# Token loop of a transformer block: order of five calls on TensorE and two on VectorE

## The chip, the cores and the metric

The kernel runs on one core of a Trainium2 chip. The metric is the device time of one execution in microseconds (us), lower is better. The engines named here are TensorE (PE in the profile, its weight loads apart as PEld), VectorE (DVE), ScalarE (ACT), GpSimd (POOL) and the DMA queues.

## The reference

The input is 32 sequences of 64 tokens, 256 wide, so 2048 tokens in 16 tiles of 128. The reference computes, in this order:

- a mixture of experts: top two of eight experts per token, three matrix products each (256 to 512 to 512 to 256);
- layer one, attention with 16 heads of 64: `q, k, v = tanh(m @ W + b)`, causal softmax, `ctx`, and `x1 = x + tanh(ctx @ Wo + bo)`;
- layer two, attention with 16 heads of 16, whose probabilities are scaled by a coherence factor and mixed with a field term (`mod = (1 - fi) * mod + fi * fa`), then `a = out @ Wout.T + bout`;
- a feed-forward step on quantised numbers: `a` is rounded in blocks of 32 to an FP4 grid, giving rows `xq`, and the result is `x1 + xq @ w_q.T + bias`.

## The kernel before

The first part computes the experts over sorted token slots. The second part, the token loop, is the subject. It takes the 16 tiles one after the other as a software pipeline written out by hand: in iteration t, TensorE does the projections, values and scores of layer one for tile t, the context of layer one for tile t-1, most of layer two for tile t-2, and the turn (transpose) of the quantised rows and the feed-forward product for tile t-3. The loop `for t in range(2, TT + 3)` at the end of TensorE's program runs t from 2 to 18; calls whose tile does not exist do nothing, so iterations 16, 17 and 18 run down with fewer and fewer calls. VectorE and ScalarE have their own lists of calls in their own loops. Every engine works its list in order, and waits on semaphores join the lists; there is no scheduler.

The calls and lines that matter:

- `l1_v(t, s)`, L870: values of layer one, tile t, sequence half s. Four matmuls in the code, two of them side by side on the two 64-column halves of the array (`tile_position=(0, r * SEQ)`), 512 columns of data each. Half 0 writes bank 3, half 1 bank 0. Half 0 waits for ScalarE's tanh of the first group of `k` projections, half 1 for that of the second.
- `l2_turn_p(t - 2, n)`, helper line L895: four turns of 128x128 of layer two's shares `p2`; n = 0 waits for the shares, n = 1 for VectorE's result of the tile before (L1889). The same helper line serves `l1_turn_p`. What is turned is copied with the field term added by VectorE's `l2_field` (L1862), for which `l2_context` (L1017) waits.
- `l2_v(t - 2)`, L980: values of layer two, on 64-column halves too; waits for VectorE's `l2_shift` (L1831). VectorE's `l2_v` (L1815) adds the bias.
- `l2_turn_q(t - 3)`, L1035: two bf16 turns of 128x128 of the quantised rows `xq`; waits for the last operation of VectorE's `l2_round` (L1416). ScalarE copies the result (`l2_xqt`, L1335), for which the product `l2_ffn` (L1044) waits.
- `l1_context` (L920) on 64x64 tiles, `l1_out` (L929), `l1_scores` (L888), the projections `l1_q` and `l1_k` (L844), the scores of layer two (L995).
- `tail_busy(t, last, n)`, L1051: n matmuls of no use, issued in iteration `last` alone: in iteration 17 the counts are 44, 12 and 26, in iteration 18 it is 84.

A 32-bit matmul of the code is two MATMUL instructions in the profile, so that `l1_v` shows x8 there and x4 in the program's order below; `l2_turn_p` is x4 in both.

Of the kernel before, what the change touches and what calls it, by code (L numbers as in the profile page):

```python
# [95 lines left out]
def exists(t, n):  # L96

    return not isinstance(t, int) or 0 <= t < n
# [12 lines left out]
def value_bank(t, s):  # L111

    return (1, 2)[s] if t == 0 else (3, 0)[s]
# [46 lines left out]
def build(nc, t_in, out):  # L160
    ctx = ExitStack()
    with ctx:
# [456 lines left out]
        def _(pe):  # L619
# [203 lines left out]
            def halves():  # L823

                return [(s, slice(s * SEQ, (s + 1) * SEQ)) for s in range(2)]

            def l1_turn_m(t):
                if not exists(t, TT):
                    return
                pe.wait_ge(m_set, t + 1)  # L830
                if t > 1:
                    pe.wait_ge(exp1_set, 2 * t)
                elif t == 0:
                    pe.wait_ge(h1t_set, SLOT_TILES)
                for k in range(KH):
                    last = pe.transpose(ps[:, turn_bank(t), k * P:(k + 1) * P], m_rows[:, k * P:(k + 1) * P], ident[:, :])
                last.then_inc(mt_ps, 1)

            def l1_project(t, wt, n):
                b = project_bank(t, n)  # L840
                for c in range(4):
                    f = (n * 4 + c) * P
                    for k in range(KH):
                        last = mm(ps[:, b, c * P:(c + 1) * P], wt[:, k, f:f + P], m_t[:, k, :],  # L844
                                  start=k == 0, stop=k == KH - 1)
                last.then_inc(qk_ps, 1)

            def l1_q(t, n):
                if not exists(t, TT):
                    return  # L850
                if n == 0:
                    pe.wait_ge(mt_set, t + 1)
                l1_project(t, wq, n)

            def l1_k(t, n):
                if not exists(t, TT):
                    return
                pe.wait_ge(qk_set, 4 * t + n + 1)
                l1_project(t, wk, n)

            def l1_v(t, s):
                if not exists(t, TT):
                    return
                if t:
                    pe.wait_ge(qk_set, 4 * t + 3 + s)
                if t == 1:
                    pe.wait_ge(exp1_set, 1 + s)
                for k in range(KH):
                    for r in range(2):
                        last = mm(ps[r * SEQ:(r + 1) * SEQ, value_bank(t, s), :], m_t[:, k, s * SEQ:(s + 1) * SEQ],  # L870
                                  wv[:, k, r * 512:(r + 1) * 512], start=k == 0, stop=k == KH - 1,
                                  tile_position=(0, r * SEQ))
                last.then_inc(v_ps, 1)
# [18 lines left out]
            def turn_p(p, bank_, n, done):  # L892
                for m in range(4):
                    h = 8 * n + 2 * m
                    last = pe.transpose(bank_[:, m * P:(m + 1) * P], p[:, h:h + 2, :], ident[:, :])  # L895
                last.then_inc(done, 1)
# [76 lines left out]
            def l2_v(t):  # L973
                if not exists(t, TT):
                    return
                pe.wait_ge(u2_set, 2 * t + 2)
                for s, q in halves():
                    for k in range(KH):
                        for r in range(2):
                            last = mm(ps[r * SEQ:(r + 1) * SEQ, 6, s * P:(s + 1) * P], x1_t[:, k, q],  # L980
                                      wv2[:, k, r * P:(r + 1) * P], start=k == 0, stop=k == KH - 1,
                                      tile_position=(0, r * SEQ))
                last.then_inc(v2_ps, 1)
# [15 lines left out]
            def l2_turn_p(t, n):  # L999
                if not exists(t, TT):  # L1000
                    return
                if n == 0:
                    pe.wait_ge(p2_set, t + 1)
                elif t:
                    pe.wait_ge(fin_set, t)
                turn_p(p2, T2[n], n, pt2_ps)
# [23 lines left out]
            def l2_turn_q(t):  # L1030
                if not exists(t, TT):
                    return
                pe.wait_ge(xq_set, t + 1)
                for k in range(KH):
                    last = pe.transpose(turned_q[:, k, :], xq[:, k * P:(k + 1) * P], ident_h[:, :])  # L1035
                last.then_inc(xqt_ps, 1)
# [11 lines left out]
            def tail_busy(t, last, n):  # L1048
                if t == last:
                    for _ in range(n):  # L1050
                        mm(bank(0, P), ident_h[:, :], ident_h[:, :], start=True, stop=True)  # L1051
# [32 lines left out]
            for t in range(2, TT + 3):  # L1084
                tail_busy(t, TT + 2, 84)
                l1_turn_m(t)
                l2_hidden(t - 2)
                l2_q_or_k(t - 2, 5, wk2)
                l1_q(t, 0)
                l2_coherence(t - 2)  # L1090
                l2_scores(t - 2)
                tail_busy(t, TT + 1, 44)
                l1_q(t, 1)
                l1_turn_p(t - 1, 0)
                l1_k(t, 0)
                l1_turn_p(t - 1, 1)
                l1_k(t, 1)
                l2_v(t - 2)
                tail_busy(t, TT + 1, 12)
                l2_turn_q(t - 3)  # L1100
                l1_context(t - 1)
                l2_ffn(t - 3)
                tail_busy(t, TT + 1, 26)
                l1_v(t, 0)
                l2_turn_p(t - 2, 0)
                l1_v(t, 1)
                l2_turn_p(t - 2, 1)
                l1_out(t - 1)
                l2_context(t - 2)
                l1_scores(t)  # L1110
                l1_turn_x1(t - 1)
                l2_out(t - 2)
                l2_q_or_k(t - 1, 4, wq2)
# [273 lines left out]
        def _(dve):  # L1387
# [242 lines left out]
            def l1_mix(t):  # L1630
                if not exists(t, TT):
                    return
                dve.wait_ge(y_gathered, 16 * TOPK * (t + 1))
                if t:
                    dve.wait_ge(mt_ps, t)
                step(ts(m_rows, yg[:, 0, :], weight_of[:, 0, t:t + 1], None, ALU.mult))
                stt(m_rows, yg[:, 1, :], weight_of[:, 1, t:t + 1], m_rows, ALU.mult, ALU.add).then_inc(m_set, 1)  # L1637
# [109 lines left out]
            def l1_v(t, s):  # L1747
                if not exists(t, TT):
                    return
                dve.wait_ge(v_ps, 2 * t + s + 1)  # L1750
                tt(v[:, s, :], bank(value_bank(t, s)), half_row("bv"), ALU.add).then_inc(vb_set, 1)
# [8 lines left out]
            def l1_sums(t):  # L1760
                if not exists(t, TT):
                    return
                step(red(z1, e1, X, ALU.add))
                step(dve.reciprocal(r1, z1))
# [90 lines left out]
            def l2_field(t, n):  # L1855
                if not exists(t, TT):
                    return
                if t == 0:
                    dve.wait_ge(field_loaded, 16)
                share = field_t[:, t:t + 1, :].to_broadcast([P, 4, P])  # L1860
                dve.wait_ge(pt2_ps, 2 * t + n + 1)
                tt(pt2[:, 4 * n:4 * n + 4, :], T2[n].rearrange("p (m q) -> p m q", m=4), share, ALU.add  # L1862
                   ).then_inc(pt2_set, 1)
# [27 lines left out]
            for t in range(0, TT + 3):  # L1891
                if t:
                    l1_mix(t)
                l2_field(t - 3, 0)
                l1_v(t - 1, 1)
                l2_field(t - 3, 1)
                l2_x1_bias(t - 3)
                l1_bias_o(t - 2)
                l1_residual(t - 2)
                l1_mask(t - 1, 0)  # L1900
                l2_bias_a(t - 3)
                l1_mask(t - 1, 1)
                l1_sums(t - 1)
                l2_scales(t - 3)
                l1_share(t - 1)
                l2_max(t - 2, 0)
                l2_z(t - 2)
                l2_max(t - 2, 1)
                l2_coherence(t - 2)
                l2_shift(t - 2, 0)  # L1910
                l2_shift(t - 2, 1)
                l2_round(t - 3)
                l2_sums(t - 2)
                l2_v(t - 2)
                l2_share(t - 2)
                l1_ctx(t - 1, 0)
                l2_result(t - 3)
                l1_v(t, 0)
                l1_ctx(t - 1, 1)
# [71 lines left out]
```

## Time and profile before

| | us |
|---|---|
| median of 3 runs | 776.12 |
| the three runs | 777.77, 776.09, 776.12 |
| the profiled execution, device time | 777.57 |
| its span, first to last instruction | 775.8 |
| PE busy | 738.0 (95%) |
| DVE busy | 497.4 (64%) |
| ACT busy | 281.0 (36%) |
| mean granted TensorE clock (1 is 2.4 GHz) | 0.98 |

The token loop takes the second half of the span, from about 320 us on. Its full iterations last close to 27 us each. A timeline row gives the start of a group of equal instructions, the time from its start to its end, the engine, the line, the operation and tiles, and in brackets the idle time ahead of it with what ended it. The end of a matmul row overlaps the start of the next, so the time that a group takes is read from start to start.

### The profile page before, as it was taken

The page shows a single profiled execution, that of the slowest core. Times are in us where ns is not written, and L with a number is a line of the kernel's source. Part 1 is how long each engine was busy: PE and PEld are TensorE (multiplying, and loading weights), DVE is VectorE, ACT ScalarE, POOL GpSimd, SP SyncE. Part 2 cuts the span into 40 slices and gives each one's busy share as a digit, 9 for nine tenths or more (in the row PEclk, how much of TensorE's full clock was granted, in tenths as well). Part 3 has the DMA queues.
Part 4 walks back from the last instruction along what each step waited for, and adds up shares of the span by engine and source line. Part 5 has one row for each costly group of instructions (what it writes and reads, how often), then busy time and mean ns, then how long its engine had stood idle before and what let it go on. Part 6 is the DMA issues. An engine that isn't in the chain of part 4 may idle for free.

```text
span 775.8 us, 22474 instructions
## 1 busy us (share of the span) xinstructions
PE 738.0 (95%) x9282; PEld 625.6 (81%) x9282; DVE 497.4 (64%) x1099; ACT 281.0 (36%) x823; POOL 84.8 (11%) x95
## 2 busy tenths in 40 slices
PE   6289999999999999999999999999999999999886
PEld 3189999569999999778977887797788779778775
DVE  3846665745444444247777877877787788678756
ACT  3032212241221221345633643563465346435420
POOL 2121112511111101110000000000000000000000
PEclk9599999999999999999999999999999999999899
DMA  9787311316110103210000000001000000000000
GB/s 317 272 270 265 131 33 44 102 42 245 41 42 29 42 22 114 78 33 5 23 29 22 10 29 29 15 16 30 22 15 23 29 22 10 29 16 9 8 9 15
DMA packets 29586, 49.27 MB, mean 64 GB/s; under 512 B 3307, under 2 KB 19051, under 8 KB 28973
## 3 DMA queue, kind: packets, MB, share of 16 engines
q1 hardware_dynamic: 20432, 32.47, 12.2%
q0 software_dynamic: 3744, 10.49, 4.5%
q10 hardware_dynamic: 5309, 4.87, 1.9%
q8 instruction: 74, 1.21, 0.7%
q14 instruction: 27, 0.22, 0.1%
HBM read 41.00 MB, written 6.82 MB: 62 GB/s over the span
## 4 chain that ended last, share of the span: by engine, by line
PE 87%; DMA 6%; DVE 4%; SPq 1%; issue 1%; ACT 1%; DVEq 0%; POOL 0%; POOLq 0%
PE ps L743 15%; PE ps L844 15%; PE ps L777 7%; PE ps L929 7%; PE ps L713 7%; PE ps L870 7%; DMA arena<-in_w 5%; PE ps L895 4%; PE ps L949 3%; PE ps L920 2%; PE ps L888 2%; PE ps L980 2%; PE ps L961 2%; PE ps L1027 2%; PE ps L995 2%; PE ps L1044 2%
## 5 line engine op out<-in xcount | busy, mean ns | idle before, releaser
L844 PE MATMUL ps<-arena,l_weights 128*128 128x128 f32 x1024 | 125.8, 276 | 0.0
L743 PE MATMUL ps<-h_t,w_now 128*128 128x128 f32 x1056 | 123.5, 275 | 1.0 <-DVE h_t L1611 1.0
L743 PEld LDWEIGHTS ps<-h_t,w_now 128*128 128x128 f32 x1056 | 120.5, 192 | 1.3 <-issue 1.2
L844 PEld LDWEIGHTS ps<-arena,l_weights 128*128 128x128 f32 x1024 | 119.3, 192 | 1.1
L1169 ACT ACTIVATE h_t<-ps,cols 128x128 f32<-128x128 f32 x132 | 37.7, 368 | 167.9 <-issue 149.4
L1586 DVE COPY w_now<-arena 128x2048 f32 x33 | 40.5, 1227 | 81.2 <-PE ps L743 70.8
L1240 ACT ACTIVATE arena<-ps,cols 128x128 f32<-128x128 f32 x256 | 73.1, 371 | 19.4 <-PE ps L844 19.4
L610 POOL DMA_INDIRECT arena<-expert_out,slot_of x32 | 30.6, 956 | 357.6 <-DVE arena L1637 308.9
L713 PEld LDWEIGHTS ps<-xg_t,w_now 128*128 128x128 f32 x528 | 63.4, 192 | 5.2 <-ACT xg_t L1152 2.6
L713 PE MATMUL ps<-xg_t,w_now 128*128 128x128 f32 x528 | 65.1, 276 | 2.0 <-DVE w_now L1572 1.5
L579 POOL DMA_INDIRECT xg<-in_x,slot_tok x36 | 41.3, 1147 | 193.4 <-PE ps L692 161.7
L777 PE MATMUL ps<-arena,h_t 128*128 x264 | 62.4, 379 | 0.0
L870 PE MATMUL ps<-l_weights,arena 128*64 128x512 f32 x256 | 61.8, 604 | 0.0
L1274 ACT ACTIVATE arena<-arena 128x256 f32<-128x256 f32 x16 | 6.7, 416 | 146.7 <-DVE arena L1783 146.7
L929 PE MATMUL ps<-l_weights,arena 128*128 128x256 f32 x256 | 58.1, 380 | 0.1
L929 PEld LDWEIGHTS ps<-l_weights,arena 128*128 128x128 f32 x256 | 47.4, 190 | 7.0 <-DVE arena L1776 1.2
L777 PEld LDWEIGHTS ps<-arena,h_t 128*128 128x128 f32 x264 | 47.6, 190 | 5.1
L895 PEld LDWEIGHTS ps<-ident,arena 128*128 128x128 f32 x256 | 29.3, 145 | 24.4 <-issue 22.7
L1572 DVE COPY w_now<-arena 128x1024 f32 x33 | 23.1, 699 | 34.0 <-PE ps L713 21.0
L895 PE MATMUL ps<-ident,arena 128*128 128x128 f32 x256 | 41.1, 286 | 0.6 <-DVE arena L1853 0.5
L1611 DVE TENSOR_SCALAR h_t<-ps,cols 128x128 f32<-128x128 f32 x132 | 37.0, 342 | 4.1 <-PE ps L743 4.0
L870 PEld LDWEIGHTS ps<-l_weights,arena 128*64 128x64 f32 x256 | 15.6, 136 | 24.4 <-issue 24.1
(301 smaller groups left out, 1110.0 us busy)
## 6 DMA issues: line engine op xcount, KB each, us to landing
arena<-in_w SPq DMA_DIRECT2D x16, 512.0 KB, 7.2
arena<-in_w SPq DMA_DIRECT2D x8, 1024.0 KB, 6.6
expert_out<-y ACTq DMA_DIRECT2D x36, 128.0 KB, 1.7
arena<-in_x_t SPq DMA_DIRECT2D x2, 1024.0 KB, 6.0
arena<-in_x SPq DMA_DIRECT2D x16, 128.0 KB, 2.3
out<-arena SPq DMA_DIRECT2D x16, 128.0 KB, 1.7
b<-in_b SPq DMA_DIRECT2D x1, 1024.0 KB, 13.1
l_weights<-in_wq SPq DMA_DIRECT2D x1, 1024.0 KB, 4.9
```

Of the source, the lines that this page charges most:

```text
L579: pool.indirect_dma_start(out=xg[j % XG][:, :], out_offset=None, in_=t_in["x"], in_offset=bass.IndirectOffsetOnAxis(ap=slot_tok[:, slot_ti ...
L713: last = mm(ps[:, 0, m * P:(m + 1) * P], w1_now[:, k, m * P:(m + 1) * P], xg_t[:, k, :], start=k == 0, stop=k == KH - 1)
L743: last = mm(ps[:, 2, m * P:(m + 1) * P], w2_now[:, k, m * P:(m + 1) * P], h1_t[j % 2][:, k, :], start=k == 0, stop=k == KM - 1)
L777: last = mm(bank(4, HID), h2_t[j % 2][:, k, :], flat[:, bass.ds(at + k * HID, HID)], start=k == 0, stop=k == KM - 1)
L844: last = mm(ps[:, b, c * P:(c + 1) * P], wt[:, k, f:f + P], m_t[:, k, :], start=k == 0, stop=k == KH - 1)
L870: last = mm(ps[r * SEQ:(r + 1) * SEQ, value_bank(t, s), :], m_t[:, k, s * SEQ:(s + 1) * SEQ], wv[:, k, r * 512:(r + 1) * 512], start=k == ...
L895: last = pe.transpose(bank_[:, m * P:(m + 1) * P], p[:, h:h + 2, :], ident[:, :])
L929: last = mm(bank(1, HID), ctx_t[:, c, :], wo[:, c, :], start=c == 0, stop=c == C1 - 1)
L1169: last = f(h1_t[j % 2][:, k, :], ps[:, 0, k * P:(k + 1) * P], ACT.Relu, bias=cols[:, bass.ds(e * KM + at + k, 1)])
L1240: last = f(dst[:, cc, :], ps[:, project_bank(t, n), c * P:(c + 1) * P], ACT.Tanh, bias=col(bias)[:, cc:cc + 1])
L1586: dve.tensor_copy(w2_now[:, :, :].rearrange("p k n -> p (k n)"), arena[:, bass.ds(at, KM * MID)]).then_inc(w2_set, 1)
L1611: last = ts(h2_t[j % 2][:, k, :], ps[:, 2, k * P:(k + 1) * P], cols[:, bass.ds(e * KM + at + k, 1)], 0.0, ALU.add, ALU.max)
```

## The change

Two pairs of calls change places in TensorE's loop, and one in VectorE's to match. Nothing is added or removed, and every call keeps its waits.

```diff
@@ TensorE, for t in range(2, TT + 3)
                 l1_turn_p(t - 1, 1)
                 l1_k(t, 1)
+                l2_turn_q(t - 3)
                 l2_v(t - 2)
                 tail_busy(t, TT + 1, 12)
-                l2_turn_q(t - 3)
                 l1_context(t - 1)
                 l2_ffn(t - 3)
                 tail_busy(t, TT + 1, 26)
                 l1_v(t, 0)
+                l1_v(t, 1)
                 l2_turn_p(t - 2, 0)
-                l1_v(t, 1)
                 l2_turn_p(t - 2, 1)
                 l1_out(t - 1)
@@ VectorE, for t in range(0, TT + 3)
                     l1_mix(t)
+                l1_v(t - 1, 1)
                 l2_field(t - 3, 0)
-                l1_v(t - 1, 1)
                 l2_field(t - 3, 1)
```

TensorE's order in a full iteration, before, from the last projection (L844) to the output of layer one (L929):

```order
L844 MATMUL ps<-arena,l_weights 128x128 x8
L980 MATMUL ps<-arena 64x128 x8
L1035 MATMUL ps<-before,arena 128x128 x2
L920 MATMUL ps<-arena 64x64 x32
L1044 MATMUL ps<-wffn,arena 128x256 x6
L870 MATMUL ps<-l_weights,arena 64x512 x4
L895 MATMUL ps<-ident,arena 128x128 x4
L870 MATMUL ps<-l_weights,arena 64x512 x4
L895 MATMUL ps<-ident,arena 128x128 x4
L929 MATMUL ps<-l_weights,arena 128x256 x8
```

The same place in the changed kernel:

```order
L844 MATMUL ps<-arena,l_weights 128x128 x8
L1035 MATMUL ps<-before,arena 128x128 x2
L980 MATMUL ps<-arena 64x128 x8
L920 MATMUL ps<-arena 64x64 x32
L1044 MATMUL ps<-wffn,arena 128x256 x6
L870 MATMUL ps<-l_weights,arena 64x512 x8
L895 MATMUL ps<-ident,arena 128x128 x8
L929 MATMUL ps<-l_weights,arena 128x256 x8
```

The turn L1035 now follows the projection, which has its shape; the two halves L870 and the two groups of turns L895 have each become one run.

TensorE's order in iteration 17, where tiles run out, before:

```order
L1051 MATMUL ps<-before 128x128 x44
L980 MATMUL ps<-arena 64x128 x8
L1051 MATMUL ps<-before 128x128 x12
L1035 MATMUL ps<-before,arena 128x128 x2
L1044 MATMUL ps<-wffn,arena 128x256 x6
L1051 MATMUL ps<-before 128x128 x26
L895 MATMUL ps<-ident,arena 128x128 x8
```

and in the changed kernel:

```order
L1051 MATMUL ps<-before 128x128 x44
L1035 MATMUL ps<-before,arena 128x128 x2
L980 MATMUL ps<-arena 64x128 x8
L1051 MATMUL ps<-before 128x128 x12
L1044 MATMUL ps<-wffn,arena 128x256 x6
L1051 MATMUL ps<-before 128x128 x26
L895 MATMUL ps<-ident,arena 128x128 x8
```

The values L980 and the twelve fillers behind them now stand behind the turn L1035 and its wait.

On VectorE, at the start of an iteration, the difference between before (-) and the changed kernel (+) is:

```order
 L1637 SCALAR_TENSOR_TENSOR arena<-arena,weight_of 128x256
-L1862 TENSOR_TENSOR arena<-ps,arena 128x512
-L1751 TENSOR_TENSOR arena<-ps,half_rows 128x512
-L1862 TENSOR_TENSOR arena<-ps,arena 128x512
+L1751 TENSOR_TENSOR arena<-ps,half_rows 128x512
+L1862 TENSOR_TENSOR arena<-ps,arena 128x512 x2
 L1798 TENSOR_TENSOR arena<-arena,rows 128x256
```

The bias of the second value half (L1751) goes ahead of the first field sum (L1862). ScalarE's order is the same.

## Rows read from the trace of the kernel before

**Rows 1.** Busy time by engine in stretches: a full iteration; iteration 16's low-clock stretch.

```profile
507.00:534.00 27.00, 27.00 (x438) 22.20 (x440) 20.64 (x44) 13.37 (x41) 1.89 (x2) 1.00 0.08 22
...
729.80:740.00 10.20, 8.05 (x99) 6.24 (x100) 9.72 (x24) 3.65 (x7) 0.00 (x0) 0.50 0.02 4
```

**Rows 2.** Timeline of PE, full iteration: values, turns, output.

```profile
524.70 1.94 PE L870 MATMUL ps<-l_weights,arena 128*64 128x512 f32 x8
526.57 0.66 PE L895 MATMUL ps<-ident,arena 128*128 128x128 f32 x4
527.16 1.94 PE L870 MATMUL ps<-l_weights,arena 128*64 128x512 f32 x8
529.03 0.66 PE L895 MATMUL ps<-ident,arena 128*128 128x128 f32 x4
529.52 3.62 PE L929 MATMUL ps<-l_weights,arena 128*128 128x256 f32 x16
```

**Rows 3.** Timeline of PE ahead of the loop: tile 0's two value halves together.

```profile
322.56 3.65 PE L870 MATMUL ps<-l_weights,arena 128*64 128x512 f32 x16
326.14 1.16 PE L888 MATMUL ps<-arena 64*64 64x64 f32 x64
```

**Rows 4.** Timeline of PE, next full iteration: projections, turns, layer two's values.

```profile
544.40 1.95 PE L844 MATMUL ps<-arena,l_weights 128*128 128x128 f32 x16
546.19 0.60 PE L895 MATMUL ps<-ident,arena 128*128 128x128 f32 x4
546.62 1.95 PE L844 MATMUL ps<-arena,l_weights 128*128 128x128 f32 x16
548.50 1.09 PE L980 MATMUL ps<-arena 128*64 128x128 f32 x16
549.53 0.28 PE L1035 MATMUL ps<-before,arena 128*128 128x128 bf16 x2
549.74 0.46 PE L920 MATMUL ps<-arena 64*64 64x64 f32 x16
```

**Rows 5.** Timeline of DVE, the same iteration: last operation of the rounding.

```profile
547.83 0.42 DVE L1416 TENSOR_TENSOR arena<-arena 128x256 bf16<-128x256 f32 x1
```

**Rows 6.** Timeline of PEld, iteration 16: weight load of the turn.

```profile
735.89 0.13 PEld L1035 LDWEIGHTS ps<-before,arena 128*128 128x128 bf16 x2 [1.18 <-DVE arena L1416]
```

**Rows 7.** Timeline of PE, iteration 16.

```profile
733.14 1.98 PE L980 MATMUL ps<-arena 128*64 128x128 f32 x16 [1.29 <-DVE arena L1831]
735.90 0.40 PE L1035 MATMUL ps<-before,arena 128*128 128x128 bf16 x2 [0.78 <-DVE arena L1416]
736.23 1.99 PE L920 MATMUL ps<-arena 64*64 64x64 f32 x64
738.15 1.46 PE L1044 MATMUL ps<-wffn,arena 128*128 128x256 bf16 x6
739.45 1.65 PE L895 MATMUL ps<-ident,arena 128*128 128x128 f32 x8
741.04 3.72 PE L929 MATMUL ps<-l_weights,arena 128*128 128x256 f32 x16
```

**Rows 8.** Timeline of DVE, iteration 16: last operation of the rounding.

```profile
735.42 0.42 DVE L1416 TENSOR_TENSOR arena<-arena 128x256 bf16<-128x256 f32 x1
```

**Rows 9.** Timeline of PE, iteration 17.

```profile
752.61 2.63 PE L1051 MATMUL ps<-before 128*128 128x128 bf16 x44
756.16 1.09 PE L980 MATMUL ps<-arena 128*64 128x128 f32 x16 [0.92 <-DVE arena L1831]
...
758.92 0.28 PE L1035 MATMUL ps<-before,arena 128*128 128x128 bf16 x2 [0.89 <-DVE arena L1416]
759.67 0.83 PE L1044 MATMUL ps<-wffn,arena 128*128 128x256 bf16 x6 [0.47 <-ACT arena L1335]
760.34 1.61 PE L1051 MATMUL ps<-before 128*128 128x128 bf16 x26
762.41 1.09 PE L895 MATMUL ps<-ident,arena 128*128 128x128 f32 x8 [0.46 <-DVE arena L1853]
```

## The prediction, made before the changed kernel was run

> **What bounds the kernel now.** I read the busy times in stretches first, since the change touches the token loop alone. In a full iteration TensorE is busy 27.00 of 27.00 us, VectorE 20.64 and ScalarE 13.37, with the clock granted in full [rows 1]. So in a full iteration time is won only by making TensorE's own sequence shorter, and the timeline of PE is the view for that: read from start to start it shows where a group of equal instructions takes longer beside one neighbour than beside another. Second comes the end of the loop. In iterations 16 and 17 TensorE has little work, its rows carry waits on VectorE in brackets, and from 729.8 to 740.0 its granted clock is 0.50, that is 1.2 GHz [rows 1, 7, 9]. There the order of the waits counts, and the price of each group depends on the clock.
>
> **Part 1, the value halves side by side, turns behind them.** Before, one half takes 526.57 - 524.70 = 1.87 us, four turns 0.59, the other half 1.87, four turns 0.49, together 529.52 - 524.70 = 4.82 us [rows 2]. What the pair costs undivided stands ahead of the loop, where tile 0's halves follow each other: 326.14 - 322.56 = 3.58 us [rows 3], 0.16 less than twice 1.87. Four turns between groups of their own full-array shape take 546.62 - 546.19 = 0.43 us [rows 4]. Eight turns behind the values are then one entry at 0.49 and four more at 0.43, 0.92 together, against 1.08. Sum: 3.58 + 0.92 = 4.50, a saving of 0.32; I take 0.30, for reading errors of 0.01 at each edge. Both pairs exist in iterations 2 to 15, so 14 x 0.30 = 4.2 us. As bounds I take 0.16 (the values alone win) and 0.34, that is 2.2 and 4.8 us.
>
> The waits that move: the second half is issued about 0.75 us earlier and needs ScalarE's last tanh of the keys. ScalarE works half of the time, and the copy L1335 that stands ahead of that tanh in its order comes earlier by part 2, so I cost it at nothing; without that cover it would be at most the 0.75. VectorE's exchange follows the new order: the bias add goes first, its input is there first, and the field sum behind it feeds L1017, which has all of L929 (3.5 us) ahead of it. The turns now start some 1.4 us later for the first group, and nobody needs the first group alone. Cost nothing.
>
> **Part 2, the turn of the quantised rows ahead of layer two's values, iterations 3 to 15.** Before, from the start of the last projection to L920 it is 549.74 - 546.62 = 3.12 us: projection 1.88, values 1.03, turn 0.21 [rows 4]. In front of a group of its own shape the same projection takes 546.19 - 544.40 = 1.79 [rows 4]. The turn now stands there, and the 0.09 of the change of shape move behind it: if the turn costs 0.11 by itself (a quarter of the four 32-bit turns' 0.43, as bf16 passes are half as many and there are half as many turns) plus 0.10 for the change, the sum is 1.79 + 0.21 + 1.03 = 3.03, a saving of 0.09 per iteration. What speaks against it is the wait. VectorE ends the rounding at 547.83 + 0.42 = 548.25 [rows 5]. From such an end to the weight load that it releases it takes 735.89 - 735.84 = 0.05 [rows 6, 8], so the load can go at 548.30, and to be hidden under the projection (which would give way at 546.62 + 1.79 = 548.41) it must go about 0.1 ahead, at 548.30 as well. There is no slack at all, but also no more than a few hundredths of delay, because VectorE's chain to this point hangs on TensorE's scores L995, and nothing between those and here is changed. I take 0.07 of 0.09: 13 x 0.07 = 0.9 us. Bounds: 0 (the load is not hidden and eats the 0.09) and 0.10, that is 0 to 1.3 us. Behind the wait stand the values, the context of layer one and the feed-forward; if the rounding came later, each hundredth would be paid in full.
>
> **Part 2 in iteration 16.** Here TensorE waits for the rounding anyway: the turn starts at 735.90, but before, L980 ran in the gap, from 733.14 on [rows 7]. Now it starts behind the turn, at 735.90 + 0.33 = 736.23. At the half clock it takes about 1.95, then L920 738.15 - 736.23 = 1.92 and L1044 739.45 - 738.15 = 1.30: the feed-forward ends at 741.4 instead of 739.45. Behind it, L929 must let the eight turns by (0.9), so 742.3 against 741.04, a loss of 1.3. If the clock is up again before the feed-forward the loss is 0.7, and none if it never falls; if the whole 1.59 from 739.45 to 741.04 repeats itself behind 741.4, it is 1.95. I take 1.3.
>
> **Part 2 in iteration 17.** Before, L980 and twelve fillers used the wait for the rounding [rows 9]. Now TensorE stands from 752.61 + 2.63 = 755.24 to 758.92, 3.7 us where the longest stand was 0.9. Then come turn, values, 12 fillers, feed-forward and 26 fillers, at full clock 0.21 + 1.03 + 12 x 0.06 + 0.67 + 26 x 0.06 = 4.2 us (fillers 2.63 / 44 = 0.06 each), and L895 starts at 763.1 instead of 762.41: a loss of 0.7. At half clock throughout the 4.2 become 4.2 x 1.9 = 8.0 (1.98 against 1.09 for L980 [rows 7, 9]) and the loss 4.5. The clock is the open question: it was low in iteration 16 while TensorE had gaps of 1.29 and 0.78 us [rows 7], and a gap of 3.7 is worse. I expect it to fall but to come back within the fillers, half-way: the low level covers 2.6 us of work and costs 1.3. I take 0.7 + 1.3 = 2.0. In iteration 18 nothing is moved.
>
> **Sum.** -4.2 - 0.9 + 1.3 + 2.0 = -1.8 us. The profiled execution took 777.57 (span 775.8 and 1.8 around it), so it would become 775.8. The median of the runs is 1.45 below this execution; the same difference taken from it gives 776.12 - 1.8 = 774.3. The gain of thirteen to fourteen full iterations, about 5, is mostly given back in the last two.
>
> **The rivals.**
>
> A, the end costs little: the clock is full when the held-back groups run. In iteration 16 the groups behind the turn would end at 735.90 + 0.21 + 1.03 + 0.96 + 0.65 = 738.75 (the last two as half of 1.92 and 1.30), ahead of the 739.45 of before, no loss; in iteration 17 it would be 0.7. Sum -4.2 - 0.9 + 0.7 = -4.4, 771.7. Against it: clock 0.50 in just that stretch, at shorter gaps [rows 1, 7]. For it: in iteration 17 of before, after the gaps of 0.92, 0.89 and 0.47, the rows still have their full-clock lengths [rows 9].
>
> B, slower: the low clock of the 3.7 us stand lasts through the fillers of iteration 17. The price is 1.3 + 4.5 = 5.8 there, and every further microsecond at half clock in the fillers of iteration 18, which before end just when the rounding does, costs 0.5. With 1.5 more the sum is -4.2 - 0.9 + 7.3 = +2.2, 778.3. The point from which it decides: if more than 7.4 us are lost at the end (5.1 of gain and 2.3 of margin), the kernel is measurably slower. For it: the low level in iteration 16 lasted 10.2 us [rows 1]. Against it: it ended while TensorE worked without gaps [rows 7], as it does in the fillers.
>
> The Trainium skill, "TensorE: Matmul & The Clock Gate", Part 1, says that the throttled state is the default and activity releases the throttle. By that rule a longer stand makes the low level in iteration 17 nearly sure, and the denser work behind it ends it; this trace agrees as far as iteration 16 goes, and by the rule alone A would be out and iteration 17 would cost between 0.7 and 4.5, nothing better than before.
>
> C, the early turn waits in full iterations: the load misses its cover and part 2 wins nothing, -4.2 + 3.3 = -0.9, 775.2. What speaks for it is the missing slack at the end of the rounding [rows 5]; against it, that the delay is a few hundredths and the same in each iteration.
>
> D, the change does not do what it says: the 0.3 per iteration does not come, because what stands between groups is not their shape but, say, the bank that they write. Then -0.9 + 3.3 = +2.4, 778.5. Against it stands the undivided pair at 3.58 [rows 3].
>
> **How the numbers follow.** From no change the measurement can tell about 0.3%, 2.3 us. Chances: my forecast 0.55 (its own spread 772.8 to 776.0, one third of it beyond the margin), A 0.20, B 0.10, C 0.12, D 0.03. Faster: 0.19 + 0.20 = 0.39. Slower: 0.08 of B and 0.02 of D, 0.10. Same: 0.51. The best sum of the bounds is -4.8 - 1.3 + 0 + 0.7 = -5.4, 770.7; the worst with part 1 as taken is -4.2 + 1.95 + 4.5 = +2.3, 778.4. No more than 2 in 10 lie beyond 771.8 and 777.6, and these I give.
>
> **What would show it.** Right: in full iterations L870 x16 taking 3.58 and the eight turns behind it 0.92, L929 0.30 nearer to the values; L1035 directly behind the projection without a bracket, or with one under 0.05; full iterations shorter by 0.3 to 0.4; in iteration 17 a bracket of 3.7 at L1035 with VectorE L1416 behind it, and a granted clock of 0.50 somewhere from there on. Wrong: the second L870 waiting for ScalarE in each iteration; a bracket of 0.1 or more at each L1035; no stretch at half clock in iteration 17 (then A), or fillers of iteration 18 longer than 0.06 each (then B).

## The result, and the profile after

| | before | changed |
|---|---|---|
| median, us | 776.16 (6 runs) | 773.33 (6 runs) |
| lowest and highest | 775.84, 777.77 | 772.08, 773.76 |
| span of the profiled execution | 775.8 | 772.0 |
| mean granted clock | 0.980 | 0.982 |

The ratio is 0.9956, 95% interval 0.9943 to 0.9969: 3.4 us less (2.4 to 4.4). Differences in us, here and below, are the ratio times the time before; the two medians themselves lie 2.8 apart. In a later session the same two kernels gave 0.9976 (0.9962 to 0.999), 1.9 us less. Both intervals lie below 1, so the changed kernel is faster, by 0.2 to 0.4 per cent; the two sizes differ by 1.5 us. Forecast were 1.8 less (774.3), inside a range of 771.8 to 777.6.

The timeline of PE in the changed kernel, a full iteration, answers to [rows 2]. The values, the turns and the output now stand like this:

```profile
521.33 3.65 PE L870 MATMUL ps<-l_weights,arena 128*64 128x512 f32 x16
524.92 1.09 PE L895 MATMUL ps<-ident,arena 128*128 128x128 f32 x8
525.85 3.62 PE L929 MATMUL ps<-l_weights,arena 128*128 128x256 f32 x16
```

From the first value half to the output it is 525.85 - 521.33 = 4.52 us, where it was 4.82: the pair takes 3.59, as tile 0's pair did [rows 3], the eight turns 0.93. That is 0.30 per iteration.

The weight loads of the same stretch (PEld) show the joint between the halves. Each half is eight loads; the first four come at once, and then two at a time while a pair of matmuls runs:

```profile
521.33 0.20 PEld L870 LDWEIGHTS ps<-l_weights,arena 128*64 128x64 f32 x4 [0.21 <-issue]
521.82 0.14 PEld L870 LDWEIGHTS ps<-l_weights,arena 128*64 128x64 f32 x2 [0.29 <-issue]
...
522.67 0.14 PEld L870 LDWEIGHTS ps<-l_weights,arena 128*64 128x64 f32 x2 [0.29 <-issue]
...
524.92 0.86 PEld L895 LDWEIGHTS ps<-ident,arena 128*128 128x128 f32 x8 [0.81 <-issue]
```

After the row at 521.82 a pair of loads comes each 0.43 us. The one at 522.67 is the first of the second half, taken in step with the others. The turns' load, in another shape, comes 0.96 after the last pair, with 0.81 of idle time ahead of it. The bracket says "issue": the profile shows no semaphore that holds it. In the kernel before, the same idle time of 0.81 stands ahead of each of the two groups of turns.

The next full iteration's projection, turn of the quantised rows and layer two's values answer to [rows 4]:

```profile
542.95 1.95 PE L844 MATMUL ps<-arena,l_weights 128*128 128x128 f32 x16
544.74 0.28 PE L1035 MATMUL ps<-before,arena 128*128 128x128 bf16 x2
544.94 1.09 PE L980 MATMUL ps<-arena 128*64 128x128 f32 x16
545.97 1.16 PE L920 MATMUL ps<-arena 64*64 64x64 f32 x64
```

From projection to context it is 545.97 - 542.95 = 3.02, where it was 3.12: 0.10 less. Together a full iteration is 544.74 - 518.25 = 26.49 us (L1035 to the next L1035) against 26.89 before (L929 at 529.52 [rows 2] to tile 15's at 717.77, seven iterations). The wait that the prediction feared did not show. VectorE's last rounding operation and TensorE's weight load for the turn, as timelines of the two engines show them:

```profile
544.16 0.42 DVE L1416 TENSOR_TENSOR arena<-arena 128x256 bf16<-128x256 f32 x1
```

```profile
544.64 0.20 PEld L1035 LDWEIGHTS ps<-before,arena 128*128 128x128 bf16 x2
```

The operation ends at 544.58, the load starts at 544.64, and its matmul at 544.74, to the hundredth when the projection gives way (542.95 + 1.79). The view of TensorE's waits over 345 to 720 us has no row for L1035 at all. It is the same in all 13 iterations: the load starts 0.05 or 0.06 after VectorE's operation ends, where before the change it was 1.26 to 1.28. The whole reserve is used up, so a further shortening of TensorE's work between the scores L995 and this turn should appear as a wait here; that was not tried.

The end of the loop answers to [rows 7] and [rows 9]. Timeline of PE in the changed kernel, iterations 16 and 17:

```profile
711.25 3.62 PE L929 MATMUL ps<-l_weights,arena 128*128 128x256 f32 x16
...
729.38 0.39 PE L1035 MATMUL ps<-before,arena 128*128 128x128 bf16 x2 [4.51 <-DVE arena L1416]
729.70 1.98 PE L980 MATMUL ps<-arena 128*64 128x128 f32 x16
731.61 1.52 PE L920 MATMUL ps<-arena 64*64 64x64 f32 x64
733.06 0.83 PE L1044 MATMUL ps<-wffn,arena 128*128 128x256 bf16 x6
733.72 0.60 PE L895 MATMUL ps<-ident,arena 128*128 128x128 f32 x4
734.66 0.66 PE L895 MATMUL ps<-ident,arena 128*128 128x128 f32 x4 [0.34 <-DVE arena L1889]
735.25 3.72 PE L929 MATMUL ps<-l_weights,arena 128*128 128x256 f32 x16
...
746.82 2.63 PE L1051 MATMUL ps<-before 128*128 128x128 bf16 x44
753.13 0.39 PE L1035 MATMUL ps<-before,arena 128*128 128x128 bf16 x2 [3.68 <-DVE arena L1416]
753.46 1.98 PE L980 MATMUL ps<-arena 128*64 128x128 f32 x16
755.36 1.29 PE L1051 MATMUL ps<-before 128*128 128x128 bf16 x12
...
757.14 1.61 PE L1051 MATMUL ps<-before 128*128 128x128 bf16 x26
758.60 1.04 PE L895 MATMUL ps<-ident,arena 128*128 128x128 f32 x8
```

TensorE stands for 4.51 and 3.68 us ahead of the moved turn, and behind each stand layer two's values take 1.98 instead of 1.09. The granted clock is 0.50 from 729.40 to 731.60 and from 753.20 to 755.30. In iteration 17 the row of 12 fillers is at half clock for its first part (1.29 for what takes 0.84), the 26 fillers are at full clock again.

In iteration 16 the late values reach TensorE by way of VectorE. VectorE adds their bias (L1815), works through its list to the result of the tile before (L1889), and TensorE's second group of turns waits for that. Timeline of DVE before, then in the changed kernel:

```profile
737.71 0.55 DVE L1815 TENSOR_TENSOR arena<-ps,half_rows 128x128 f32<-128x128 f32 x2
...
739.91 0.47 DVE L1889 SCALAR_TENSOR_TENSOR arena<-ps,act_inv,arena 128x256 f32<-128x256 f32 x1
```

```profile
731.79 0.68 DVE L1815 TENSOR_TENSOR arena<-ps,half_rows 128x128 f32<-128x128 f32 x2 [0.64 <-PE ps L980]
...
734.13 0.48 DVE L1889 SCALAR_TENSOR_TENSOR arena<-ps,act_inv,arena 128x256 f32<-128x256 f32 x1
```

Counted from tile 15's L929, L1889 starts at 22.14 before and at 22.88 after. These 0.74 are the 0.73 by which tile 16's L929 is late.

Spans compare badly here, because the part ahead of the loop ends earlier or later from one execution to the next (last section). So the kernels are compared by stages, from start to start of rows in the profiled executions: a full iteration; iteration 16 from tile 15's L929 to tile 16's; iteration 17 from there to its L895. From that row to the end all the kernels of this document have 13.3 to 13.5.

| kernel | full iteration | iteration 16 | iteration 17 |
|---|---|---|---|
| before | 26.89 | 23.27 | 21.37 |
| changed | 26.49 | 24.00 | 23.35 |
| changed, later session | 26.49 | 24.92 | 23.54 |

So 14 x 0.30 + 13 x 0.10 = 5.5 us are won in the full iterations, and 0.73 + 1.98 = 2.7 (later 1.65 + 2.17 = 3.8) lost in the last two: -2.8 and -1.7, beside the measured -3.4 and -1.9.

### The profile page after: what moved, and what is told of

Read it like the earlier page. It is cut to its first block, busy times and chain, and to the rows that moved or that the text cites. A ratio compares the mean times of both kernels' runs of the same rounds, so it can differ in the third digit from the quotient of the medians.

```text
span 772.0 us, 22474 instructions
## 1 busy us (share of the span) xinstructions
PE 730.5 (95%) x9282; PEld 626.5 (81%) x9282; DVE 497.3 (64%) x1099; ACT 280.6 (36%) x823; POOL 84.7 (11%) x95
## 4 chain that ended last, share of the span: by engine, by line
PE 90%; DVE 6%; issue 1%; ACT 1%; DMA 1%; POOL 1%; DVEq 0%; POOLq 0%; ACTq 0%
PE ps L743 15%; PE ps L844 15%; PE ps L713 8%; PE ps L777 7%; PE ps L929 7%; PE ps L870 7%; PE ps L895 4%; PE ps L949 3%; PE ps L980 2%; PE ps L920 2%; PE ps L888 2%; PE ps L961 2%; PE ps L1027 2%; PE ps L995 2%; PE ps L1017 2%; PE ps L1044 1%
## 5 line engine op out<-in xcount | busy, mean ns | idle before, releaser
L844 PE MATMUL ps<-arena,l_weights 128*128 128x128 f32 x1024 | 125.8, 276 | 0.0
L743 PE MATMUL ps<-h_t,w_now 128*128 128x128 f32 x1056 | 123.5, 275 | 1.0 <-DVE h_t L1611 1.0
L743 PEld LDWEIGHTS ps<-h_t,w_now 128*128 128x128 f32 x1056 | 120.5, 192 | 1.3 <-issue 1.2
L844 PEld LDWEIGHTS ps<-arena,l_weights 128*128 128x128 f32 x1024 | 119.3, 192 | 1.1
L870 PE MATMUL ps<-l_weights,arena 128*64 128x512 f32 x256 | 58.7, 599 | 0.0
L929 PE MATMUL ps<-l_weights,arena 128*128 128x256 f32 x256 | 58.1, 380 | 0.1
L929 PEld LDWEIGHTS ps<-l_weights,arena 128*128 128x128 f32 x256 | 47.4, 190 | 7.0 <-DVE arena L1776 1.2
L870 PEld LDWEIGHTS ps<-l_weights,arena 128*64 128x64 f32 x256 | 16.9, 136 | 30.0 <-issue 29.7
L1611 DVE TENSOR_SCALAR h_t<-ps,cols 128x128 f32<-128x128 f32 x132 | 37.0, 343 | 4.1 <-PE ps L743 4.0
L895 PEld LDWEIGHTS ps<-ident,arena 128*128 128x128 f32 x256 | 28.6, 141 | 12.7 <-issue 11.4
L895 PE MATMUL ps<-ident,arena 128*128 128x128 f32 x256 | 36.9, 276 | 0.7 <-DVE arena L1889 0.3
```

The source lines that it names most:

```text
L743: last = mm(ps[:, 2, m * P:(m + 1) * P], w2_now[:, k, m * P:(m + 1) * P], h1_t[j % 2][:, k, :], start=k == 0, stop=k == KM - 1)
L929: last = mm(bank(1, HID), ctx_t[:, c, :], wo[:, c, :], start=c == 0, stop=c == C1 - 1)
L1611: last = ts(h2_t[j % 2][:, k, :], ps[:, 2, k * P:(k + 1) * P], cols[:, bass.ds(e * KM + at + k, 1)], 0.0, ALU.add, ALU.max)
```

## The experiments

**Each part alone.** `v_only` has the value halves side by side, with VectorE's exchange, and leaves the turn of the quantised rows where it was:

```diff
-                l2_turn_q(t - 3)
                 l2_v(t - 2)
                 tail_busy(t, TT + 1, 12)
+                l2_turn_q(t - 3)
```

> Part 1 alone (value halves side by side, VectorE's exchange with it); the turn of the quantised rows stays behind layer two's values. Theory: each of 14 full iterations is 0.30 shorter and the end is as before, so -4.2 us against the kernel before, about 771.9, and L929 of tile 15 to L929 of tile 16 lasts 23.27 as before (24.00 in the changed kernel). Rival (part 2 is what wins, part 1's 0.3 is lost elsewhere): no more than -1.

`q_only` is the other half of the change:

```diff
                 l1_v(t, 0)
-                l1_v(t, 1)
                 l2_turn_p(t - 2, 0)
+                l1_v(t, 1)
                 l2_turn_p(t - 2, 1)
```

(and VectorE's two calls back in their old order).

> Part 2 alone: the turn of the quantised rows in front of layer two's values in every iteration, the value halves apart as before. Theory: 13 full iterations win 0.11 each (1.4 us), iterations 16 and 17 lose 0.7 and 2.0, so +1.3 us, about 777.4; the projection, the turn and the values take 1.78 + 0.21 + 1.02. Rival (the two parts help each other, the early turn only pays with the halves together): the full iterations win nothing and the total is +2.7.

Measured against the kernel before in the same session (777.69): `v_only` 773.42, ratio 0.9954 (0.9938 to 0.997), -3.6 us; `q_only` 779.13, ratio 1.0018 (1.0004 to 1.0032), +1.4 us; -4.2 and +1.3 were expected. The kernel before was at 776.1 to 777.7 in the different sessions, so expectations given as times are compared by their distance from it. By stages:

| kernel | full iteration | iteration 16 | iteration 17 |
|---|---|---|---|
| v_only | 26.59 | 23.58 | 21.45 |
| q_only | 26.79 | 24.41 | 23.51 |

The two parts do not help each other: 0.30 and 0.10 add up to the 0.40 of both. Iteration 16 of `v_only` is 23.58 where 23.27 was expected (last section). Alone, the second part makes the kernel slower, and its rows say where. Timeline of PE in `q_only`, iteration 16's and 17's waits:

```profile
735.60 0.39 PE L1035 MATMUL ps<-before,arena 128*128 128x128 bf16 x2 [4.06 <-DVE arena L1416]
...
759.76 0.28 PE L1035 MATMUL ps<-before,arena 128*128 128x128 bf16 x2 [3.68 <-DVE arena L1416]
759.97 1.49 PE L980 MATMUL ps<-arena 128*64 128x128 f32 x16
761.39 1.46 PE L1051 MATMUL ps<-before 128*128 128x128 bf16 x12
```

Here the clock falls only inside L980 (1.49), so the low stretch lies over later groups than in the changed kernel. The loss of iteration 17 is nearly the same, 2.1.

**The old order at the end.** `old_end` is the changed kernel except in iterations 16 to 18:

```diff
-                l2_turn_q(t - 3)
+                if t < TT:
+                    l2_turn_q(t - 3)
                 l2_v(t - 2)
                 tail_busy(t, TT + 1, 12)
+                if t >= TT:
+                    l2_turn_q(t - 3)
```

> The changed kernel, but in iterations 16 to 18 the turn of the quantised rows stays behind layer two's values and the twelve fillers, as before. Theory: the 5.5 us of the full iterations stay and the 2.7 of the end come back: -5.5 against before, about 770.6, the stand of 3.7 us in iteration 17 is gone and its L980 takes 1.09. Rival (the end is later for another reason, such as the clock following from the shorter iterations): no faster than the changed kernel, 773.3.

Measured 772.05 against 777.69, ratio 0.993 (0.9911 to 0.995), -5.4 us. The stages are 26.49, 23.44 and 21.27. Timeline of PE in `old_end`, iteration 17:

```profile
752.29 1.09 PE L980 MATMUL ps<-arena 128*64 128x128 f32 x16 [0.92 <-DVE arena L1834]
...
755.05 0.28 PE L1035 MATMUL ps<-before,arena 128*128 128x128 bf16 x2 [0.89 <-DVE arena L1419]
```

The stand is split again into two short ones, and the values take 1.09. What the changed kernel lost at its end is given back but for 0.1, so the loss came from the order in these two iterations and what that order brings with it.

**Keeping the array at work through the stands.** Two things are in that loss: groups held back behind the wait, and the half clock they then run at. `fill_stands` keeps the changed order and fills the wait with matmuls that compute nothing of use:

```diff
+                tail_busy(t, TT, 75)
+                tail_busy(t, TT + 1, 60)
                 l2_turn_q(t - 3)
                 l2_v(t - 2)
```

> The changed kernel with matmuls of no use ahead of the moved turn, 75 in iteration 16 and 60 in iteration 17, to keep TensorE working while it waits for the rounding. If the half clock behind the stands makes part of the loss, L980 and the groups behind it take their full-clock times (1.09 instead of 1.98), iteration 16 loses nothing and iteration 17 only the 0.7 of the order: about 2.0 less than the changed kernel, 771.3. Rival (the loss is the order alone, clock or not): 773.3, or more if the fillers outlast the wait.

Measured 772.71 against 777.69, ratio 0.9941 (0.9922 to 0.996), -4.6 us. The time is nearer to the rival's 773.3 than to 771.3, but the kernel before is 1.5 higher here than the 776.16 from which both were reckoned; measured from there, -4.6 is close to the -4.9 of 771.3. The traces show it without the sessions' spread. Timeline of PE:

```profile
723.64 4.35 PE L1051 MATMUL ps<-before 128*128 128x128 bf16 x75
728.32 0.28 PE L1035 MATMUL ps<-before,arena 128*128 128x128 bf16 x2 [0.33 <-DVE arena L1418]
728.53 1.09 PE L980 MATMUL ps<-arena 128*64 128x128 f32 x16
...
745.03 5.98 PE L1051 MATMUL ps<-before 128*128 128x128 bf16 x104
751.34 0.28 PE L1035 MATMUL ps<-before,arena 128*128 128x128 bf16 x2 [0.33 <-DVE arena L1418]
751.55 1.09 PE L980 MATMUL ps<-arena 128*64 128x128 f32 x16
```

and the busy times of the two stretches, where the figure behind POOL's is the granted clock, 1.00 in both:

```profile
723.60:733.50 9.90, 8.84 (x174) 7.58 (x172) 9.45 (x23) 3.17 (x6) 0.00 (x0) 1.00 0.01 2
745.00:755.40 10.40, 10.07 (x176) 9.53 (x168) 9.48 (x22) 1.82 (x4) 0.00 (x0) 1.00 0.01 3
```

Iteration 16 lasts 23.27 as before the change, though its values still stand behind the turn: at full clock they are done at 729.56, ahead of VectorE's bias add at 730.13 (L1817 in this kernel), which has no bracket. So there the later order costs nothing by itself, and the whole loss needs the half clock. Iteration 17 lasts 21.91, 0.54 over before: there the order costs 0.5 and the clock the other 1.4.

**VectorE's exchange.** `v_pe_only` keeps the changed order on TensorE and puts VectorE's two calls back:

```diff
-                l1_v(t - 1, 1)
                 l2_field(t - 3, 0)
+                l1_v(t - 1, 1)
```

> The changed kernel with VectorE's order as before (first field sum ahead of the bias of the second value half). Theory: the gain is TensorE's; VectorE then waits for the first group of turns, which ends about 1.4 us later than before, but L1017 behind the field sums has over 3 us of cover, so 773.3, the same as the changed kernel. Rival (the exchange on VectorE carries part of the gain, since the bias frees what the scores wait for): 14 iterations at 0.1 to 0.3 longer, 774.7 to 777.5.

Measured 774.65 against 777.39, ratio 0.9964 (0.9951 to 0.9978), -2.8 us. The run time alone does not decide, since 774.65 lies at the rival's lower edge (774.7) and the changed kernel itself gave -3.4 and -1.9. The full iteration does: 544.91 - 518.43 = 26.48, the changed kernel's, where the rival asked for 0.1 to 0.3 more. Timeline of DVE in `v_pe_only`, then in the changed kernel:

```profile
525.79 0.69 DVE L1862 TENSOR_TENSOR arena<-ps,arena 128x512 f32<-128x512 f32 x1 [0.22 <-PE ps L895]
...
529.68 0.42 DVE L1783 TENSOR_TENSOR arena<-ps,rows 128x256 f32<-128x256 f32 x1 [1.67 <-PE ps L929]
```

```profile
525.31 0.68 DVE L1751 TENSOR_TENSOR arena<-ps,half_rows 128x512 f32<-128x512 f32 x1
...
529.50 0.42 DVE L1783 TENSOR_TENSOR arena<-ps,rows 128x256 f32<-128x256 f32 x1 [1.98 <-PE ps L929]
```

Without the exchange VectorE waits 0.22 for the first turns, and has 0.31 less to wait for L929 (1.67 instead of 1.98). The exchange is not needed for the gain.

**What the joint between the halves costs.** In `split_full` one bf16 matmul of no use, in the full 128x128 shape, stands between the halves, in `split_half` two of 64 columns side by side, in the shape of the values themselves:

```diff
                 l1_v(t, 0)
+                between(t)
                 l1_v(t, 1)
```

```
split_full: mm(bank(0, P), ident_h[:, :], ident_h[:, :], start=True, stop=True)
split_half: for r in range(2):
                mm(ps[r * SEQ:(r + 1) * SEQ, 0, 0:P], ident_h[:, r * SEQ:(r + 1) * SEQ], ident_h[:, :],
                   start=True, stop=True, tile_position=(0, r * SEQ))
```

Ahead of these lines both have the check that the tile exists, and the wait of the second half itself, which so moves ahead of the inserted matmuls.

> The changed kernel with one extra bf16 matmul of no use between the two value halves, in the full 128x128 shape. Theory (what the pair saves is the change of array shape and back): 0.056 for the matmul and 0.30 for the two changes, 14 times, so +4.9 us, about 778.2. Rival (the saving comes from the turns, not from the shape): 0.06 x 14, +0.8, 774.1.

> The same with two extra matmuls of 64 columns each, side by side in the shape of the value halves, in place of the one in full shape. Theory: no change of shape, so only their own time, 0.06 to 0.11 each iteration: +0.8 to +1.5 us, 774.1 to 774.8, and the second half's first weights are loaded ahead. Rival (any foreign group between the halves ends the overlap): as dear as the full-shape one, about 778.

Measured in one session, before at 777.39: `split_full` 778.62, ratio 1.002 (1.0008 to 1.0031); `split_half` 775.95, ratio 0.9984 (0.9969 to 0.9999). Timeline of PE in `split_full`, then in `split_half` (the numbers of lines below the insertion move by 6 and 8):

```profile
523.89 1.94 PE L870 MATMUL ps<-l_weights,arena 128*64 128x512 f32 x8
525.76 0.23 PE L879 MATMUL ps<-before 128*128 128x128 bf16 x1
525.92 1.94 PE L870 MATMUL ps<-l_weights,arena 128*64 128x512 f32 x8
527.79 1.09 PE L901 MATMUL ps<-ident,arena 128*128 128x128 f32 x8
```

```profile
523.52 1.94 PE L870 MATMUL ps<-l_weights,arena 128*64 128x512 f32 x8
525.28 0.23 PE L880 MATMUL ps<-before 128*64 128x128 bf16 x2
525.34 1.89 PE L870 MATMUL ps<-l_weights,arena 128*64 128x512 f32 x8
527.16 1.09 PE L903 MATMUL ps<-ident,arena 128*128 128x128 f32 x8
```

From the values to the turns it is 3.90 with the full shape between and 3.64 with the half shape, against 3.59 with nothing. The same 128 columns of data cost 0.31 in one shape and 0.05 in the other, so 0.26 is the change of shape, out and back; besides the shape, the two differ only in being one matmul or two side by side. Part of it is seen at the first half: with a full-shape group behind it, it takes 525.76 - 523.89 = 1.87 as in [rows 2], with a half-shape one 525.28 - 523.52 = 1.76. This is the Trainium skill's rule in "TensorEngine Tiling (Array Packing)", Tiling Modes, that changing the tiling mode, not just the tile, drains the engine; the runs here agree, and put 0.26 to 0.30 on a pair of such changes around a 512-column group.

By stages `v_pe_only` and the two split kernels are:

| kernel | full iteration | iteration 16 | iteration 17 |
|---|---|---|---|
| v_pe_only | 26.49 | 24.60 | 23.51 |
| split_full | 26.80 | 24.65 | 23.49 |
| split_half | 26.55 | 24.37 | 23.50 |

The full iterations are 0.31 and 0.06 longer than the changed kernel's 26.49, which over 14 iterations is 4.3 and 0.8 us. `split_half` was expected 1.3 to 2.0 below the kernel before and is 1.2 below (0.1 to 2.4): its inserted matmuls cost what was expected, and iteration 16 lost 1.1 here instead of 0.7.

**The best version.** Last, in one session, the old end again, the old end with fillers in iteration 16, and the changed kernel:

```diff
+                tail_busy(t, TT, 20)
                 l2_v(t - 2)
+                tail_busy(t, TT, 25)
                 tail_busy(t, TT + 1, 12)
```

(on top of `old_end`'s edit, for `old_end_filled`).

> The changed kernel with the old order in iterations 16 to 18, and in iteration 16 also 20 matmuls of no use ahead of layer two's values and 25 behind them. Theory: what is left to win at the end is the half clock of iteration 16; with TensorE kept at work L980, L920 and L1044 take full-clock times and L929 of tile 16 comes 23.3 us after that of tile 15, where 23.27 to 23.6 were seen at half clock. Since VectorE's chain bounds this iteration, that is worth 0 to 0.3 us beside the kernel with the old end alone: -5.5 to -5.8 against the kernel before. Rival (the fillers stand in the way of the values or of the turn): iteration 16 longer than 23.6.

> The kernel with the old order in iterations 16 to 18 once more, beside the one with fillers and on the same chip: -5.5 us against the kernel before, ratio 0.993. Rival: its first result was helped by the spread of that session (774.9 to 779.6 for the kernel before), and it is at the changed kernel's 0.9956.

> The changed kernel once more, on the same chip as the two with the old end: ratio 0.9956 to 0.9963, so that the old end is worth 2 to 2.7 us beside it. Rival: no difference between them.

| kernel | median, us | ratio to before (776.78) | iteration 16 | iteration 17 |
|---|---|---|---|---|
| old_end_filled | 771.14 | 0.9931 (0.9916 to 0.9946) | 23.28 | 21.36 |
| old_end_again | 771.80 | 0.9928 (0.9911 to 0.9945) | 23.54 | 21.26 |
| after_again | 774.91 | 0.9976 (0.9962 to 0.999) | 24.92 | 23.54 |

The old end is at 0.993 twice, faster than both kernels of the study, by 5.4 to 5.6 us against before. Beside the changed kernel it is worth 3.1 by the medians of these runs and 3.7 by stages, more than the expected 2 to 2.7, as iteration 16 of the changed kernel lost 1.65 here. The fillers in iteration 16 lift the clock there to 1.00 and shorten it by 0.26 in the trace, but iteration 17 takes 0.1 back, and the runs do not tell the two apart.

## Why the prediction was right, step by step

- **Part 1, 0.30 per iteration:** measured 0.30, undivided pair 3.59 (3.58 taken from the rows ahead of the loop), turns 0.93 (0.92). 14 of them make the 4.2. The rival D is out: with the shape kept, a foreign group between the halves costs 0.05.
- **Its hidden costs, at nothing:** right. No wait on ScalarE at the second half. Between 345 and 720 us the view of TensorE's waits has two entries, 0.6 on ScalarE (L949) and 0.3 on VectorE (L937), once each, and the kernel before has the same two. The cover on VectorE was larger than needed, since even without the exchange nothing is lost. The first turns start 3.59 - 1.87 = 1.7 later after the values' start, not 1.4, which changes nothing.
- **Part 2 in full iterations, 0.07:** a size was off. The change of shapes came out at 0.10 (0.09 from the rows), and I took 0.02 away for a wait that never appeared. 1.3 instead of 0.9 us. The load goes at the last possible moment, 0.05 or 0.06 after VectorE's operation ends in each of the 13 iterations, as the prediction had worked out, so rival C was near without coming true.
- **Iteration 16, a loss of 1.3:** the size was near, the path was not the one described. The six traces with this order and no fillers lost 0.73, 1.65, 1.14, 1.33, 1.38 and 1.10, on average 1.2. The prediction added up TensorE's own groups: turn, values, context, feed-forward, eight turns. In the first trace that sum gives almost no loss, since with L920 at 1.45 and the feed-forward at 0.66 from start to start, the eight turns would have let L929 by only 0.1 later than before. What held L929 was VectorE's L1889, which the prediction did not have: its chain waited 0.64 for the late values. In the second trace L1889 waited 0.67 for the feed-forward as well. That the clock decides was foreseen ("none if it never falls"), and `fill_stands` bears it out. The case "the loss is 0.7" if the clock is up before the feed-forward was also summed wrongly, it gives 0.6; that 0.73 was measured is luck.
- **Iteration 17, 0.7 + 1.3:** measured 1.98 and 2.17, split by `fill_stands` into 0.5 for the order and 1.4 for the clock. Four more traces of this order lost 2.12 to 2.14. I had written that the clock would fall and come back within the fillers; it was back at the latest within the 26 fillers in each trace of this order. How long the low level would last was a guess, half-way between two bounds, and it held.
- **The sum:** -1.8 forecast, -2.8 and -1.7 by stages, -3.4 and -1.9 by the runs. "Faster by over 0.3%" had 0.39 and "same" 0.51: the first session's ratio lies beyond that margin, the second's not quite. By stages the first execution gained 0.4 more in part 2 and lost 0.6 less in iteration 16 than forecast, and both point the same way. That the second came out at the forecast is partly luck: the 0.4 more of part 2 stands against 0.35 more lost in iteration 16.
- **Rivals A and B:** A (the end costs little) and B (the clock stays low into iteration 18) are both out by the traces: the 84 fillers take 4.85 in every one, and each trace of the changed order without fillers at the waits has a low stretch in both iterations. B's own price was +2.2, just inside the margin of 2.3 that was set for slower, so its 0.08 for slower asked for more than the case as described gives. In the second trace of the changed kernel iteration 17's L980 did take 1.09, but the low stretch then lay over the groups behind it (the 26 fillers took 2.34), at about the same total.

## What to carry to other kernels

Where TensorE is busy all the time, count the changes of array shape in its order, and put groups of one shape together: the profile shows each as a start-to-start time that depends on the neighbour, and a pair of changes cost 0.26 to 0.30 us here. A move that wins in the full iterations of a pipeline has to be priced again in its last ones, where the same wait is no longer covered: look at what now stands behind the wait, who else needs it (here VectorE), and give those iterations their own order. The longer stand of TensorE cost twice here, 0.5 for the work held back in iteration 17, and 0.7 to 1.7 in each of the last two iterations for the half clock behind it.

## What the runs showed that was not expected

The part ahead of the loop, untouched by any of the edits, ends at different times. Its last long row in two traces (timeline of PE; the changed kernel, and the same kernel in the later session):

```profile
318.24 3.73 PE L844 MATMUL ps<-arena,l_weights 128*128 128x128 f32 x32
```

```profile
320.28 3.73 PE L844 MATMUL ps<-arena,l_weights 128*128 128x128 f32 x32
```

That is 2 us between two executions of the same kernel, as much as the effect in question, and it would account for a good part of the spread of the runs (772.31 to 776.82 for the changed kernel in the later session). This is not shown, since only one execution of each kernel and session has a trace. The two traces do say where their 2.04 us arise: 0.81 of it by the first L743 that waits (55.13 and 55.94), and 1.00 in a wait of L743 for VectorE's L1611 at 139.17 that the first trace does not have. What sets these two off was not tried.

In iteration 16 the half clock costs the kernel before nothing that can be seen: it has 23.27 with the clock at 0.50 [rows 1], and `old_end_filled` has 23.28 with it at full. VectorE's chain bounds the iteration there, with its L1889 at 22.14 or 22.15 after tile 15's L929 in both, and TensorE has time to be slow, until the changed order makes that chain wait for the values. Yet `old_end` and `v_only` lose 0.2 to 0.3 in the same iteration with L1889 in the same place. There the low stretch lies later, over the four turns behind L1889: the granted clock in them is 0.50 in `v_only` (735.10 to 736.00) and 1.00 in the kernel before (740.40 to 741.00).
